# Cross-attention and FP4 feed-forward on one core: three transfers between engines re-ordered, PSUM banks dealt anew

## The chip, the cores and the metric

One core of a Trainium2 chip. Its engines run their own queues in order and wait for one another on semaphores: TensorE (PE, matrix products and transposes), VectorE (DVE), ScalarE (ACT), GpSimd (POOL) and SyncE (SP, which issues the transfers here). PE writes to PSUM, which has eight banks of 128x512 float32; this kernel names all eight. The metric is the device time of one execution in microseconds.

## What is computed

`x` is (4, 1024, 256), the context (4, 154, 192), 16 heads of 64, the hidden width of the feed-forward 704. Cut to what matters:

```python
def xattn(x, context, Wq, Wk, Wv, Wo, bo):           # x is layer-normed
    q, k, v = x @ Wq, context @ Wk, context @ Wv      # 16 heads of 64
    attn = softmax(einsum('bhnd,bhmd->bhnm', q, k) * 64 ** -0.5)
    return merge_heads(attn @ v) @ Wo + bo

def ffn(x, w_gate, w_up, w_down):                     # x is layer-normed
    lin = lambda x, w: fp4(x) @ fp4(w).T              # fp4: quantise and dequantise blocks of 16
    return lin(silu(lin(x, w_gate)) * lin(x, w_up), w_down)

x = x + xattn(layernorm(x), ctx_768, ...)             # its result, a tile of it, is x1 below
x = x + ffn(layernorm(x), ...)
```

## The kernel before, in words

The 4096 rows of `x` are 32 tiles of 128. One *step* works on four tiles at once, at different stages: tile t has its attention computed (16 heads as 8 *pairs* u), tile e = t-1 finishes its attention and gets x1, tile f = t-2 goes through gate and up, tile d = t-3 through down. A step has 8 *slots* k, and each engine has its own list of what it does in slot k, in a fixed order written out in a function `step` per engine. Steps come in pairs (`par` 0 for even tiles, 1 for odd ones); the function `schedule` calls them: six steps in line, a loop over the batches 1 to 3 with four steps that also make K, V and the product B of V and Wo for the new batch (set-ups "v", "k", "roll", "settle") and an inner loop of two pairs of plain steps, and two last steps, then four that only drain.

The products that need more than one float32r pass come as a high part, which ACT copies out of PSUM (`hi_part`), and a low part, which DVE forms as the difference (`lo_part`).

A pair u of heads of tile t passes through the engines so:

- PE, slot u: `scores` (L967) into a bank of PSUM, three products.
- DVE, slot u: `negmax`, the maximum of each head (L782).
- ACT, slot u: exp of the two heads (L610), with sums. Next slot: DVE inverts the sums (L746), POOL multiplies (`normalise`, L472).
- PE, slot u+2: `turn_probs` (L979), which transposes the weights, two blocks of 128 columns for even u and three for odd u, into a bank of PSUM.
- ACT, first work of slot u+3: `weights_hi` makes `pT_hi`. DVE, slot u+3, behind `invert_sums` and ahead of `negmax` of that slot: `weights_lo` makes `pT_lo` (L741 by L637).
- PE, slot u+4, just behind the scores: `attend` (L988), 6 or 9 products with B that gather in the bank `ps_o` over the eight pairs of a tile.

Counts past 7 run on into the next step. When the last `attend` of tile e is done, in slot 3 of step t, DVE adds its result to the input rows: `x1 = xr + ps_o` (L804). The first `attend` of tile t, in slot 4, writes `ps_o` anew and waits for that add. ACT first copies the old `x1` to `y` (L628), before the add may overwrite it.

In the kernel before, the scores of even and odd pairs have a bank each (`ps_s[u % 2]`), so that scores wait for the exp two pairs back; the transposed weights have one bank (`ps_t`), so that `turn_probs(u)` waits for `pT_lo` of pair u-1. PE's order in a slot is: scores, `attend`, `turn_probs`, then transposes for the feed-forward (slots 1, 4, 5), transposes of the next input (slot 6 of even steps), `gate_up` (slots 2 to 5), `down_product` (slot 7), a `q_product` (slots 0, 1, 2, 4 of even steps and 0, 1, 3, 6 of odd ones), the set-up's jobs. In even steps `down_product` waits for `xT_lo`, DVE's work in slot 7 behind `negmax`. DVE's `xqT_lo` (slot 2) and `hqT_lo` (slots 5, 6) stand between `weights_lo` and `negmax`. DVE does the add of x1 in slot 4, behind `negmax` and `q_lo`.

Of the kernel before, what the change touches and what calls it, by code (L numbers as in the profile page):

```python
# [23 lines left out]
def xattn_ffn_kernel(nc: bass.Bass, x, ctx_768, Wq, Wk, Wv, Wo, bo, w_gate, w_up, w_down, out):  # L24
# [29 lines left out]
    with ExitStack() as stack:  # L54
# [69 lines left out]
        ps_t, ps_q, ps_o, ps_m = (bank(n) for n in ("ps_t", "ps_q", "ps_o", "ps_m"))  # L124
        ps_s = [bank("ps_s0"), bank("ps_s1")]
# [4 lines left out]
        def ctx_bank(r):  # L130
            return (ps_s[0], ps_s[1], ps_t, ps_g[0], ps_o)[r]
# [379 lines left out]
        def _(act):  # L511
# [60 lines left out]
            def weights_hi(t, u):  # L572
                if some(PAIRS * t + u - 1):
                    act.wait_ge(o_mm, PAIRS * t + u - 1)
                hi_part(pT[u % 2][0][:, 0:blocks(u), :], parts(ps_t, blocks(u)), (t_mm, PAIRS * t + u + 1), pT_hi)

            def step(pair, par, own=True, before=True, gate=True, down=True, out_=True, ahead=True, queries=True,
# [3 lines left out]
                for k in range(SLOTS):  # L581
# [24 lines left out]
                    if own:  # L606
                        act.wait_ge(max_v, PAIRS * t + k + 1)
                        for s in range(2):
                            h = 2 * k + s
                            ins = act.activation(probs[:, h, 0:M], ps_s[k % 2][:, s * M:(s + 1) * M], ACT.Exp,  # L610
# [12 lines left out]
                    if down and k == 3:  # L623
# [9 lines left out]
        def _(dve):  # L633
# [105 lines left out]
            def weights_lo(t, u):  # L739
                n = blocks(u)  # L740
                lo_part(pT[u % 2][1][:, 0:n, :], parts(ps_t, n), pT[u % 2][0][:, 0:n, :],  # L741
# [19 lines left out]
            def step(pair, par, own=True, before=True, gate=True, down=True, out_=True, ahead=True, queries=True,  # L761
# [3 lines left out]
                for k in range(SLOTS):  # L765
# [14 lines left out]
                    if own:  # L780
                        dve.wait_ge(s_mm, PAIRS * t + k + 1)
                        dve.tensor_reduce(negmax[:, 2 * k:2 * k + 2],  # L782
                                          ps_s[k % 2][:, 0:UM].rearrange("p (h m) -> p h m", h=2),
# [13 lines left out]
                    if before and k == 4:  # L797
                        dve.wait_ge(o_mm, PAIRS * (e + 1))
                        dve.wait_ge(xr_p, e + 1)
                        if some(d + 1):  # L800
                            dve.wait_ge(y_a, d + 1)
                        elif not some(e):
                            dve.wait_ge(raw_mm, RAW_T[3])
                        dve.tensor_tensor(x1[1 - par], xr[1 - par][:, :], ps_o[:, 0:C], ALU.add).then_inc(x1_v, 1)  # L804
# [19 lines left out]
                    if before and k == 5:  # L824
# [6 lines left out]
                        dve.tensor_scalar(xri[:, :], xri[:, :], TIES_DOWN, None, ALU.mult).then_inc(xq_v, 1)  # L831
                    if gate and k == 6:
                        dve.wait_ge(h_v, Q * (f + 1))
                        largest(eh[:, 0:F], hri[:, :], hq_v)
# [18 lines left out]
        def _(pe):  # L853
# [113 lines left out]
            def scores(t, pair, par, u, setup):  # L967
# [3 lines left out]
                if some(PAIRS * t + u - 1):  # L971
                    pe.wait_ge(exp_a, PAIRS * t + u - 1)
                terms = ((1, 0), (0, 1), (0, 0))
                for i, (a, b) in enumerate(terms):
                    ins = pe.matmul(ps_s[u % 2][:, 0:UM], q_sb[a][:, u, par * P:(par + 1) * P], K_sb[b][:, u, :],  # L975
# [3 lines left out]
            def turn_probs(t, u):  # L979
                pe.wait_ge(norm_p, PAIRS * t + u + 1)  # L980
                if some(PAIRS * t + u):
                    pe.wait_ge(pT_lo, PAIRS * t + u)
# [124 lines left out]
```

## Time and profile before

| | |
|---|---|
| median of 3 runs | 984.53 us (983.6 to 984.84) |
| the profiled execution | 986.75 us |
| its span, first to last instruction | 984.9 us |
| PE, DVE, ACT, POOL busy | 857.0, 757.5, 534.0, 529.5 us |
| mean granted TensorE clock | 0.973 of full speed |

The engines overlap, so their busy times don't add up to the span. A row of the view in order of time gives the start of an instruction, its length, engine, line, operation and tiles, and in brackets the idle time of its engine just before and what ended it. Matrix products are pipelined: each is recorded as longer than the distance to the next.

### The profile page before, as it was taken

How to read it: one execution, taken by the hardware profiler on the slowest of the kernel's cores; microseconds unless marked ns; L12 is line 12 of the kernel's file. 1: busy time of each engine (PE TensorE's matmuls, PEld its weight loads, DVE VectorE, ACT ScalarE, POOL GpSimd, SP SyncE). 2: the span in 40 equal slices, each digit the busy share in tenths (PEclk: the TensorE clock that was granted, in tenths of full speed). 3: DMA queues.
4: the chain of work that ended last, by engine and by line, in shares of the span. 5: the costliest groups of instructions: out<-in, count | busy, mean ns of one | idle time of the engine just before them, and what ended most of it. 6: DMA issues, size and time to landing. Idle time of an engine off the chain costs nothing.

```text
span 984.9 us, 21389 instructions
## 1 busy us (share of the span) xinstructions
PE 857.0 (87%) x6254; PEld 812.8 (83%) x6254; DVE 757.5 (77%) x2176; ACT 534.0 (54%) x1879; POOL 529.5 (54%) x677
## 2 busy tenths in 40 slices
PE   4786789999999999989989999989999999999874
PEld 3666789988888998888978888889888888888863
DVE  5857788877778888867878888876877888887762
ACT  4454455556565555556555555556555555655520
POOL 2545666554535656545554656554553656555651
PEclk9888999999999999999999999999999999999986
DMA  7101000001010000001000000001000000000000
GB/s 215 39 11 49 7 17 13 22 13 44 7 33 17 13 23 11 21 14 39 12 28 23 12 22 12 21 8 33 23 7 23 12 18 12 16 11 12 7 11 11
DMA packets 19869, 23.13 MB, mean 23 GB/s; under 512 B 2642, under 2 KB 18234, under 8 KB 19770
## 3 DMA queue, kind: packets, MB, share of 16 engines
q1 hardware_dynamic: 19770, 21.94, 7.2%
q8 instruction: 47, 0.77, 0.3%
q14 instruction: 52, 0.43, 0.1%
HBM read 17.74 MB, written 4.19 MB: 22 GB/s over the span
## 4 chain that ended last, share of the span: by engine, by line
PE 63%; DVE 21%; issue 8%; ACT 4%; POOL 2%; DMA 1%; DVEq 1%; SPq 0%; POOLq 0%; ACTq 0%
PE ps_g L1015 10%; PE ps_q L937 8%; PE ps_s L975 8%; PE ps_t L985 5%; PE ps_o L998 5%; PE ps_o L1000 5%; PE ps_o L999 5%; DVE negmax L782 3%; DVE pT_lo L637 3%; PE ps_m L865 3%; PE ps_g L900 3%; PE ps_m L1025 3%; PE ps_m L1027 2%; PE ps_m L1026 2%; DVE scales L667 2%
## 5 line engine op out<-in xcount | busy, mean ns | idle before, releaser
L472 POOL TENSOR_TENSOR probs<-probs,rsum 128x308 f32<-128x308 f32 x256 | 180.0, 703 | 284.2 <-DVE rsum L746 283.6
L610 ACT ACTIVATE probs<-ps_s,negmax 128x154 f32<-128x154 f32 x512 | 194.7, 386 | 229.4 <-DVE negmax L782 228.2
L998 PE MATMUL ps_o<-B_sb,pT_lo 128*128 128x256 f32 x640 | 183.6, 287 | 38.5 <-DVE x_both L804 33.9
L782 DVE TENSOR_REDUCE negmax<-ps_s 128x2 f32<-128x308 f32 x256 | 121.3, 474 | 78.4 <-PE ps_s L975 76.6
L1000 PE MATMUL ps_o<-B_sb,pT_hi 128*128 128x256 f32 x640 | 181.2, 283 | 0.0
L999 PE MATMUL ps_o<-B_sb,pT_hi 128*128 128x256 f32 x640 | 180.9, 283 | 0.0
L998 PEld LDWEIGHTS ps_o<-B_sb,pT_lo 128*128 128x128 f32 x640 | 121.7, 190 | 45.3 <-issue 42.9
L637 DVE TENSOR_TENSOR pT_lo<-ps_t,pT_hi 128x256 fp32r<-128x256 f32 (+1 forms) x256 | 122.7, 479 | 42.6 <-ACT pT_hi L514 37.4
L985 PE MATMUL ps_t<-ident,probs 128*128 128x128 f32 x640 | 115.0, 278 | 35.9 <-DVE pT_lo L637 35.3
L1015 PE MATMUL ps_g<-WGU,xqT_hi 128*128 128x352 f32 x512 | 136.6, 349 | 3.5 <-DVE B_sb L637 1.9
L514 ACT ACTIVATE pT_hi<-ps_t 128x256 fp32r<-128x256 f32 (+1 forms) x256 | 111.4, 435 | 29.1 <-PE ps_t L985 22.7
L1000 PEld LDWEIGHTS ps_o<-B_sb,pT_hi 128*128 128x128 f32 x640 | 122.1, 191 | 0.0
L999 PEld LDWEIGHTS ps_o<-B_sb,pT_hi 128*128 128x128 f32 x640 | 121.8, 190 | 0.0
L985 PEld LDWEIGHTS ps_t<-ident,probs 128*128 128x128 f32 x640 | 73.8, 141 | 47.3 <-issue 45.7
L610 ACT ACTIVATION_READ_ACCUMULATOR probs<-ps_s,negmax 128x1 f32 x512 | 100.9, 197 | 0.0
L975 PE MATMUL ps_s<-K_hi,q_lo 128*128 128x308 f32 x256 | 87.1, 340 | 3.6 <-issue 3.6
L1015 PEld LDWEIGHTS ps_g<-WGU,xqT_hi 128*128 128x128 f32 x512 | 85.3, 194 | 4.9 <-issue 2.6
L937 PE MATMUL ps_q<-xT_hi,Wq_lo 128*128 128x256 f32 x256 | 80.7, 315 | 8.7 <-DVE q_lo L637 6.1
L1015 PE MATMUL ps_g<-WGU,xqT_lo 128*128 128x352 f32 x256 | 83.5, 326 | 0.0
L441 POOL TENSOR_TENSOR hn<-hn,hc 128x704 f32<-128x704 f32 x32 | 54.4, 1700 | 50.8 <-DVE hc L692 50.8
L975 PE MATMUL ps_s<-K_hi,q_hi 128*128 128x308 f32 x256 | 78.4, 306 | 0.0
L975 PE MATMUL ps_s<-K_lo,q_hi 128*128 128x308 f32 x256 | 78.1, 305 | 0.0
(149 smaller groups left out, 2236.7 us busy)
## 6 DMA issues: line engine op xcount, KB each, us to landing
xa<-in_x_dram SPq DMA_DIRECT2D x33, 128.0 KB, 2.1
xr<-in_x_dram SPq DMA_DIRECT2D x32, 128.0 KB, 2.0
out_dram<-y_xn SPq DMA_DIRECT2D x32, 128.0 KB, 1.7
W_sb<-in_L_xattn_Wk_dram SPq DMA_DIRECT2D x4, 512.0 KB, 4.4
W_sb<-in_L_xattn_Wv_dram SPq DMA_DIRECT2D x3, 512.0 KB, 3.6
probs<-in_L_xattn_Wq_dram SPq DMA_DIRECT2D x1, 1024.0 KB, 7.0
Wo_sb<-in_L_xattn_Wo_dram SPq DMA_DIRECT2D x1, 1024.0 KB, 6.6
VT<-in_ctx_dram SPq DMA_DIRECT2D x1, 384.0 KB
```

The lines of the kernel that those rows point to most:

```text
L472: pool.tensor_tensor(unit, unit, rsum[:, 2 * u:2 * u + 2].unsqueeze(2) .to_broadcast([P, 2, M]), ALU.mult).then_inc(norm_p, 1)
L514: act.activation(dst, src, ACT.Copy).then_inc(done, 1)
L610: ins = act.activation(probs[:, h, 0:M], ps_s[k % 2][:, s * M:(s + 1) * M], ACT.Exp, bias=negmax[:, h:h + 1], accum_out=sums[:, h:h + 1])
L637: dve.tensor_tensor(dst, src, hi.bitcast(F32), ALU.subtract).then_inc(done, 1)
L782: dve.tensor_reduce(negmax[:, 2 * k:2 * k + 2], ps_s[k % 2][:, 0:UM].rearrange("p (h m) -> p h m", h=2), AX_X, ALU.max, negate=True).then_ ...
L937: ins = pe.matmul(ps_q[:, 0:2 * P], Wq_sb[w][:, k, u * P:(u + 1) * P], xT[x_][:, k, :], start=(i == 0), stop=(i == len(terms) - 1))
L975: ins = pe.matmul(ps_s[u % 2][:, 0:UM], q_sb[a][:, u, par * P:(par + 1) * P], K_sb[b][:, u, :], start=(i == 0), stop=(i == len(terms) - 1))
L985: ins = pe.transpose(ps_t[:, j * P:(j + 1) * P], probs_rows[:, at:at + P], ident[:, :])
L998: pe.matmul(ps_o[:, 0:C], lo[:, j, :], w[:, 0:C], start=first, stop=False)
L999: pe.matmul(ps_o[:, 0:C], hi[:, j, :], w[:, C:2 * C], start=False, stop=False)
L1000: ins = pe.matmul(ps_o[:, 0:C], hi[:, j, :], w[:, 0:C], start=False, stop=last)
L1015: ins = pe.matmul(ps_g[q % 2][:, 0:2 * QF], x_[:, k, :], WGU[:, k, a, :, q * QF:(q + 1) * QF], start=(i == 0), stop=(i == len(terms) - 1))
```

## The change

Three things. DVE's add of x1 goes from slot 4, behind `negmax` and `q_lo`, to the end of slot 3; ACT's copy of the old x1 to `y` goes from slot 3 to slot 2. PE's `turn_probs` goes from just behind `attend` to the end of the slot's products, behind the feed-forward's transposes, `gate_up`, `down_product`, `q_product` and the jobs, and ahead of the chunks of raw weights that the first steps turn. The scores now have one bank, so that scores wait for the exp of the pair before; the transposed weights have two, so that `turn_probs(u)` waits for `pT_lo` of pair u-2. The orders of ACT and DVE are otherwise as they were.

```diff
--- before.py
+++ after.py
@@ -121,14 +121,14 @@
         def bank(name):
             return stack.enter_context(nc.psum_tensor(name, [P, 512], F32))
 
-        ps_t, ps_q, ps_o, ps_m = (bank(n) for n in ("ps_t", "ps_q", "ps_o", "ps_m"))
-        ps_s = [bank("ps_s0"), bank("ps_s1")]
+        ps_s, ps_q, ps_o, ps_m = (bank(n) for n in ("ps_s", "ps_q", "ps_o", "ps_m"))
+        ps_t = [bank("ps_t0"), bank("ps_t1")]
         ps_g = [bank("ps_g0"), bank("ps_g1")]
         BANKS = {"q": ps_q, "0": ps_g[0], "1": ps_g[1]}
         FIRST_K = "0101"
 
         def ctx_bank(r):
-            return (ps_s[0], ps_s[1], ps_t, ps_g[0], ps_o)[r]
+            return (ps_s, ps_t[0], ps_t[1], ps_g[0], ps_o)[r]
 
         ld_ctx, ld_w, ld_wkv, ld_wo, ld_wq, ld_bo = (
             sem(n) for n in ("ld_ctx", "ld_w", "ld_wkv", "ld_wo", "ld_wq", "ld_bo"))
@@ -572,7 +572,7 @@
             def weights_hi(t, u):
                 if some(PAIRS * t + u - 1):
                     act.wait_ge(o_mm, PAIRS * t + u - 1)
-                hi_part(pT[u % 2][0][:, 0:blocks(u), :], parts(ps_t, blocks(u)), (t_mm, PAIRS * t + u + 1), pT_hi)
+                hi_part(pT[u % 2][0][:, 0:blocks(u), :], parts(ps_t[u % 2], blocks(u)), (t_mm, PAIRS * t + u + 1), pT_hi)
 
             def step(pair, par, own=True, before=True, gate=True, down=True, out_=True, ahead=True, queries=True,
                      setup=None):
@@ -607,7 +607,7 @@
                         act.wait_ge(max_v, PAIRS * t + k + 1)
                         for s in range(2):
                             h = 2 * k + s
-                            ins = act.activation(probs[:, h, 0:M], ps_s[k % 2][:, s * M:(s + 1) * M], ACT.Exp,
+                            ins = act.activation(probs[:, h, 0:M], ps_s[:, s * M:(s + 1) * M], ACT.Exp,
                                                  bias=negmax[:, h:h + 1], accum_out=sums[:, h:h + 1])
                         ins.then_inc(exp_a, 1)
                     if own and ahead and k == 4:
@@ -620,7 +620,7 @@
                            .then_inc(xln2_a, 1)
                     if turn_at(t, k, 0) is not None:
                         chunk_hi(turn_at(t, k, 0))
-                    if down and k == 3:
+                    if down and k == 2:
                         at = pair - 2 + par
                         act.wait_ge(x1_v, d + 1)
                         if some(at):
@@ -738,7 +738,7 @@
 
             def weights_lo(t, u):
                 n = blocks(u)
-                lo_part(pT[u % 2][1][:, 0:n, :], parts(ps_t, n), pT[u % 2][0][:, 0:n, :],
+                lo_part(pT[u % 2][1][:, 0:n, :], parts(ps_t[u % 2], n), pT[u % 2][0][:, 0:n, :],
                         (pT_hi, PAIRS * t + u + 1), pT_lo)
 
             def invert_sums(t, u):
@@ -780,7 +780,7 @@
                     if own:
                         dve.wait_ge(s_mm, PAIRS * t + k + 1)
                         dve.tensor_reduce(negmax[:, 2 * k:2 * k + 2],
-                                          ps_s[k % 2][:, 0:UM].rearrange("p (h m) -> p h m", h=2),
+                                          ps_s[:, 0:UM].rearrange("p (h m) -> p h m", h=2),
                                           AX_X, ALU.max, negate=True).then_inc(max_v, 1)
                     if out_ and k == 0:
                         dve.wait_ge(d_mm, c + 1)
@@ -795,13 +795,6 @@
                     if turn_at(t, k, 1) is not None:
                         chunk_lo(turn_at(t, k, 1))
                     if before and k == 4:
-                        dve.wait_ge(o_mm, PAIRS * (e + 1))
-                        dve.wait_ge(xr_p, e + 1)
-                        if some(d + 1):
-                            dve.wait_ge(y_a, d + 1)
-                        elif not some(e):
-                            dve.wait_ge(raw_mm, RAW_T[3])
-                        dve.tensor_tensor(x1[1 - par], xr[1 - par][:, :], ps_o[:, 0:C], ALU.add).then_inc(x1_v, 1)
                         if some(e):
                             dve.wait_ge(xln2_a, e)
                         stats(x1[1 - par], st2, mv2, ve2, nm2, (x1_v, e + 1), ln2_v, 5 * e)
@@ -829,6 +822,14 @@
                         fp4_scales(xri[:, :], xsc[:, :], xri[:, :], xq_v, 6 * e)
                         dve.wait_ge(xq_v, 6 * e + 3)
                         dve.tensor_scalar(xri[:, :], xri[:, :], TIES_DOWN, None, ALU.mult).then_inc(xq_v, 1)
+                    if before and k == 3:
+                        dve.wait_ge(o_mm, PAIRS * (e + 1))
+                        dve.wait_ge(xr_p, e + 1)
+                        if some(d + 1):
+                            dve.wait_ge(y_a, d + 1)
+                        elif not some(e):
+                            dve.wait_ge(raw_mm, RAW_T[3])
+                        dve.tensor_tensor(x1[1 - par], xr[1 - par][:, :], ps_o[:, 0:C], ALU.add).then_inc(x1_v, 1)
                     if gate and k == 6:
                         dve.wait_ge(h_v, Q * (f + 1))
                         largest(eh[:, 0:F], hri[:, :], hq_v)
@@ -968,21 +969,21 @@
                 pe.wait_ge(q_lo, PAIRS * pair + u + 1)
                 if setup and setup[0] in ("start", "roll"):
                     pe.wait_ge(k_lo, KV * setup[1] + u // 2 + 1)
-                if some(PAIRS * t + u - 1):
-                    pe.wait_ge(exp_a, PAIRS * t + u - 1)
+                if some(PAIRS * t + u):
+                    pe.wait_ge(exp_a, PAIRS * t + u)
                 terms = ((1, 0), (0, 1), (0, 0))
                 for i, (a, b) in enumerate(terms):
-                    ins = pe.matmul(ps_s[u % 2][:, 0:UM], q_sb[a][:, u, par * P:(par + 1) * P], K_sb[b][:, u, :],
+                    ins = pe.matmul(ps_s[:, 0:UM], q_sb[a][:, u, par * P:(par + 1) * P], K_sb[b][:, u, :],
                                     start=(i == 0), stop=(i == len(terms) - 1))
                 ins.then_inc(s_mm, 1)
 
             def turn_probs(t, u):
                 pe.wait_ge(norm_p, PAIRS * t + u + 1)
-                if some(PAIRS * t + u):
-                    pe.wait_ge(pT_lo, PAIRS * t + u)
+                if some(PAIRS * t + u - 1):
+                    pe.wait_ge(pT_lo, PAIRS * t + u - 1)
                 for j in range(blocks(u)):
                     at = b_at(u, j) * P
-                    ins = pe.transpose(ps_t[:, j * P:(j + 1) * P], probs_rows[:, at:at + P], ident[:, :])
+                    ins = pe.transpose(ps_t[u % 2][:, j * P:(j + 1) * P], probs_rows[:, at:at + P], ident[:, :])
                 ins.then_inc(t_mm, 1)
 
             def attend(t, u, setup):
@@ -1039,10 +1040,6 @@
                         attend(e, k + PAIRS - 4, setup if kind == "settle" else None)
                     if own and k >= 4:
                         attend(t, k - 4, setup if kind in ("start", "roll") else None)
-                    if before and k < 2:
-                        turn_probs(e, k + PAIRS - 2)
-                    if own and k >= 2:
-                        turn_probs(t, k - 2)
                     if gate and k == 1:
                         pe.wait_ge(xq_p, 4 * f + 4)
                         m_free((y_v, d), (xqT_lo, f + 1))
@@ -1073,6 +1070,10 @@
                             pe.wait_ge(q_lo, PAIRS * (pair + par) + max(made))
                     for job in jobs_at(setup, k):
                         make(job, setup[1])
+                    if before and k < 2:
+                        turn_probs(e, k + PAIRS - 2)
+                    if own and k >= 2:
+                        turn_probs(t, k - 2)
                     if turn_at(t, k, 0) is not None:
                         chunk_transposes(turn_at(t, k, 0))
 
```

## Rows read from the trace of the kernel before

**Rows 1.** The page, its line of busy time by engine.

```profile
PE 857.0 (87%) x6254; PEld 812.8 (83%) x6254; DVE 757.5 (77%) x2176; ACT 534.0 (54%) x1879; POOL 529.5 (54%) x677
```

**Rows 2.** The waits: engine, line, releaser; total us, times, longest.

```profile
PE ps_t L985 <- DVE pT_lo L637: 35.3, 40, 3.2
PE ps_o L998 <- DVE x_both L804: 33.9, 28, 2.4
```

**Rows 3.** PE in order of time, an even step; start us, us, instruction.

```profile
610.57 0.31 PE L975 MATMUL ps_s<-K_hi,q_lo 128*128 128x308 f32 x1
...
612.64 0.30 PE L975 MATMUL ps_s<-K_hi,q_lo 128*128 128x308 f32 x1
...
615.38 0.31 PE L975 MATMUL ps_s<-K_hi,q_lo 128*128 128x308 f32 x1
...
618.41 0.30 PE L975 MATMUL ps_s<-K_hi,q_lo 128*128 128x308 f32 x1
...
621.21 0.30 PE L975 MATMUL ps_s<-K_hi,q_lo 128*128 128x308 f32 x1
...
622.79 0.36 PE L998 MATMUL ps_o<-B_sb,pT_lo 128*128 128x256 f32 x1 [0.99 <-DVE x_both L804]
...
623.58 0.38 PE L985 MATMUL ps_t<-ident,probs 128*128 128x128 f32 x2
...
625.81 0.30 PE L975 MATMUL ps_s<-K_hi,q_lo 128*128 128x308 f32 x1
...
634.40 0.38 PE L1025 MATMUL ps_m<-WD,hqT_lo 128*128 128x256 f32 x1 [0.38 <-DVE xT_lo L637]
...
636.64 0.30 PE L975 MATMUL ps_s<-K_hi,q_lo 128*128 128x308 f32 x1
```

**Rows 4.** PE in order of time, the odd step before it.

```profile
585.52 0.31 PE L975 MATMUL ps_s<-K_hi,q_lo 128*128 128x308 f32 x1
...
592.65 0.30 PE L975 MATMUL ps_s<-K_hi,q_lo 128*128 128x308 f32 x1
...
596.16 0.30 PE L975 MATMUL ps_s<-K_hi,q_lo 128*128 128x308 f32 x1
...
598.06 0.36 PE L998 MATMUL ps_o<-B_sb,pT_lo 128*128 128x256 f32 x1 [1.32 <-DVE x_both L804]
...
600.36 0.30 PE L975 MATMUL ps_s<-K_hi,q_lo 128*128 128x308 f32 x1
```

**Rows 5.** ACT in order of time, the even step and the next.

```profile
624.06 0.38 ACT L514 ACTIVATE pT_hi<-ps_t 128x256 fp32r<-128x256 f32 x1 [0.37 <-PE ps_t L985]
...
637.77 0.39 ACT L610 ACTIVATE probs<-ps_s,negmax 128x154 f32<-128x154 f32 x1 [2.76 <-DVE negmax L782]
...
640.77 0.49 ACT L514 ACTIVATE pT_hi<-ps_t 128x384 fp32r<-128x384 f32 x1
```

**Rows 6.** DVE in order of time, the same stretch.

```profile
622.23 0.41 DVE L804 TENSOR_TENSOR x_both<-xr,ps_o 128x256 f32<-128x256 f32 x1
...
624.86 0.56 DVE L637 TENSOR_TENSOR hqT_lo<-ps_m,hqT_hi 128x384 fp32r<-128x384 f32 x1
626.43 0.48 DVE L782 TENSOR_REDUCE negmax<-ps_s 128x2 f32<-128x308 f32 x1 [1.01 <-PE ps_s L975]
...
630.44 0.47 DVE L782 TENSOR_REDUCE negmax<-ps_s 128x2 f32<-128x308 f32 x1
...
633.28 0.47 DVE L782 TENSOR_REDUCE negmax<-ps_s 128x2 f32<-128x308 f32 x1
...
637.26 0.48 DVE L782 TENSOR_REDUCE negmax<-ps_s 128x2 f32<-128x308 f32 x1 [0.66 <-PE ps_s L975]
...
638.65 0.17 DVE L746 RECIPROCAL rsum<-sums 128x2 f32<-128x2 f32 x1 [0.15 <-ACT probs L610]
...
641.77 0.42 DVE L637 TENSOR_TENSOR xqT_lo<-ps_m,xqT_hi 128x256 fp32r<-128x256 f32 x1
```

**Rows 7.** The core, its span and its mean granted clock.

```profile
core 0: 984.9 us, clock 0.973
```

## The prediction

> **What bounds the kernel now.** I read the page first: TensorE (PE) is busy 857.0 us of a span of 984.9, VectorE (DVE) 757.5, ScalarE (ACT) 534.0 [rows 1]. A busy share does not say who waits for whom, so the waits come next. In the whole span PE stands still 35.3 us before the transposes of the weights, for DVE's `pT_lo`, and 33.9 us before the first product of `attend`, for DVE's `x1` [rows 2]. These two are what the change goes for. What it must not lengthen is seen only in the order of time, so I lay the three engines of one ordinary pair of steps beside each other.
>
> Call S(k) the start of PE's scores in slot k and N(k) the start of DVE's `negmax` in that slot. The step of an even tile runs from 610.57 to 636.64, 26.07 us; that of an odd tile from 585.52 to 610.57, 25.05 us [rows 3, 4]. In slots 0 to 3 PE is the last to finish: S goes 2.07, 2.74, 3.03, 2.80 us from slot to slot [rows 3], and DVE's `negmax` starts 0.62 us after the scores (N(5) is 626.43, S(5) 625.81 [rows 3, 6]). In slot 4 PE stands until `x1` is there: the add starts at 622.23 and takes 0.41, and the product starts at 622.79, 0.15 us behind its end [rows 3, 6]. From N(5) on, DVE is the last: N(6) is N(5)+4.01, N(7) is N(6)+2.84, and `down_product`, which needs `xT_lo` in even steps, starts at N(7)+1.12 [rows 3, 6]. So the step is PE-bound in its first half and DVE-bound in its second.
>
> **The change part by part.**
>
> *x1 earlier.* The same 0.41 us instruction runs one slot earlier on DVE, so nothing is added. Queued behind it are `invert_sums(3)` and `pT_lo` of slot 4; these wait for ACT's `pT_hi` anyway, which covers the 0.41 us; without that cover it would cost 0.41. PE's wait in slot 4 goes: it is from the end of the scores to 622.79, about 1.2 us in the even step (621.21+0.43), and 598.06-596.60, about 1.46, in the odd one [rows 3, 4]. ACT's copy of `y` moves a slot ahead with it and has idle time there; I cost it at nothing, at most its own length.
>
> *Transposes last.* The same instructions, the same number. PE no longer waits for the previous `pT_lo` (two banks), and the 35.3 us go from that place. But what hangs on them comes later. ACT's first work in slot k is `pT_hi(k-3)`, and DVE's `pT_lo(k-3)` stands ahead of `negmax(k)` in its queue; the diff leaves both orders as they are. The trace has the lags: the transposes of two blocks start at 623.58 and `pT_hi` at 624.06, 0.48 later [rows 3, 5]. Two transposes take about 0.22 (0.11 each, an estimate from the 18 products that fill 634.40 to 636.64), so `pT_hi` starts 0.26 us after PE is done with the slot. The next DVE instruction behind `pT_lo` starts 0.80 after `pT_hi` for two blocks (624.06 to 624.86) and 1.00 for three (640.77 to 641.77) [rows 5, 6]. So where the transposes end the slot, `negmax` starts 1.06 or 1.26 us after PE is free, not 0.62. In slot 2 `xqT_lo` (0.42) stands between, in slot 5 `hqT_lo` (0.56) [rows 6]: 1.68 and 1.62. The records of DVE overlap the next by a little, so these two are upper ends.
>
> *One bank for the scores.* Scores(k+1) now need exp(k). `negmax` at 637.26 gives exp at 637.77 (+0.51), and DVE sees exp's end at 638.65 (+0.88) [rows 5, 6]. How soon PE starts after an ACT release is in no row of this place; the nearest is 0.15 us after DVE's `x1`. The bounds are 0 and 0.3; I take 0.11, so that S(k+1) is not before N(k)+1.50.
>
> *Sum, even step*, from S(0)=0, with the transposes of the slot before just done:
> N(0)=1.26. S(1) = the later of 2.07 (PE) and 2.76 (exp) = 2.76: a new stall of 0.69. N(1)=3.4 (scores +0.62; `pT_hi` runs right behind exp, whose end by the +0.88 is at 2.65, and `negmax` may start 0.80 after that, at 3.45). S(2)=2.76+2.74=5.50. N(2)=5.50+1.68=7.18. S(3) = the later of 8.53 and 8.68 = 8.68. N(3)=8.53+1.06=9.59. S(4) = the later of 11.48 and 11.09 = 11.48. N(4)=11.40 to 11.48+1.26=12.74. `x1` is there at about N(3)+1.8=11.4, before scores(4) end at 11.9: no wait. S(5)=11.48+(4.60-1.20)=14.88. N(5)=14.88+1.62=16.50. Before, N(5) was 626.43-610.57=15.86: already 0.64 later, though 1.2 was saved. Then as before N(6)=20.51 and N(7)=23.35. Scores(7) wait for exp(6) to 22.0, which hides, since PE then waits for `xT_lo`: down starts at 24.47, takes 2.24, and the transposes, now behind it, 0.33: the next S(0) is 27.04. That is +0.97 us.
>
> *Odd step*: the same to S(3)=8.68; slot 3 is 3.51 long (596.16-592.65 [rows 4]), S(4)=12.19, N(4)=13.45, S(5) = the later of 12.19+4.20-1.46=14.93 and 14.95, N(5)=16.55, N(6)=20.56, S(7)=22.06 by exp. The scores and three blocks of `attend` take about 1.5 (an estimate, 0.12 a product), down 2.24, transposes 0.33: 26.13, that is +1.08.
>
> Sixteen of the 32 steps with scores of their own are of these two kinds. Mean +1.0 each: +16 us. In the other steps (the first two, the four that make K, V and B of each batch, the last two) slots are longer, so the exp wait often hides while the `x1` gain stays. Bounds: each gains 1.2 (-19 in all) or loses 1.0 (+16). I take 0: the long slots gain, the short ones among them lose. The sum is 984.9+16, about 1001; the profiled execution itself took 986.75, the median of the runs is 984.53, so **1000** in the runs' terms.
>
> A rule that speaks against the change: DVE's `negmax` starts with the scores' bank at 637.26 and ACT's exp holds it to about 638.6, while in the kernel before PE may fill the other bank [rows 5, 6]. The Trainium skill, "Perfetto Trace Analysis", section "Matmuls", says that independent groups should rotate through different PSUM banks, so that emptying one overlaps the next group's matmuls. By that rule alone the scores would lose their overlap and the transposes gain it. No figure follows from it here.
>
> **The rivals.**
> *Faster.* The lag behind the transposes doesn't reach `negmax` (N stays at S+0.62). Then S goes 0, 2.12, 4.86, 7.89, 10.69, 14.09 and N(5)=14.71, 1.15 us earlier than before; 0.33 is given back behind down. 28 steps had the wait [rows 2]: 28x0.8, about 962 us. For it: PE's records show these two waits as its largest. Against: `pT_lo` is ahead of `negmax` in DVE's queue. The point from which it decides: slots 0, 2 and 5 each hand their lag on, so if each lag were 0.33 us shorter than I have it (N(0) at S(0)+0.93), the even step would come out even, and below that the kernel is faster.
> *Nothing to measure.* Gain and lag cancel, 983 to 986, for instance when the twelve setup and edge steps gain all of their 1.2.
> *Dearer than forecast.* Scores(7) at N(6)+1.5 and slot 6 meet more late work on DVE (its second half is full), or `x1` is late in slot 3 and PE keeps about 0.5 us of its wait: another 0.5 to 0.8 a step on 28, 1015 to 1023.
> *The clock falls.* PE stands more often. With waits of 1.3 us in each step the granted clock stays at its upper level (mean 0.973 over the run [rows 7]); were half of the matmuls to run at 1.2 GHz, hundreds of us would be lost. I see no gap longer than about 1.5 us in the sum.
>
> **How the numbers follow.** Forecast (986.5 to 1015): 0.70. Dearer: 0.12, with the clock in it 0.02. Even: 0.05. Faster: 0.13, most of it near 962 to 982. The median of this kernel is told from no change at about 0.2%, 2 us. So slower 0.82, same 0.05, faster 0.13. The range leaves out 2 in 10: from the lower edge of "even" to the middle of "dearer", 980 to 1019. The likeliest case's own is 988 to 1013.
>
> **What would show it.** Right: PE's waits for `x1` and `pT_lo` are gone from the list; in their place PE waits before scores for ACT's exp, in slots 0 and 7 above all, and DVE's waits for `pT_hi` grow; N(0) near S(0)+1.3, N(5) near S(5)+1.6, N(5) to N(6) still 4.0; steps near 27.0 and 26.1. Wrong: N near S+0.62 in slots 0, 4 and 5, or slot 7 shorter than now, or steps of the batch set-up that lose several us, which I did not lay out slot by slot.

## The result

The changed kernel took 1022.25 us at the median (1021.7 to 1026.87 in four executions; a fifth took 1018.79), against 984.1 for the kernel before on the same chip: a ratio of 1.0388 (95% interval 1.0352 to 1.0424; the brackets behind later ratios are such intervals). It is slower, as forecast, but by 38 us and not by 16, and outside the range of 980 to 1019. The profiled execution has a span of 1025.0 us, 40.1 more than before; all lengths of steps and stretches below are from such profiled executions. Its mean granted clock is 0.974, where it was 0.973 [rows 7].

The page's line of busy time of the changed kernel, which answers to [rows 1]:

```profile
PE 872.4 (85%) x6254; PEld 815.3 (80%) x6254; DVE 722.9 (71%) x2176; ACT 524.4 (51%) x1879; POOL 530.5 (52%) x677
```

DVE and ACT do the same work in less busy time and a longer span. The waits of the changed kernel (engine, line, releaser; total us, times, longest):

```profile
ACT pT_hi L514 <- PE ps_t L986: 220.4, 175, 4.5
...
DVE pT_lo L637 <- ACT pT_hi L514: 196.2, 160, 3.3
...
PE ps_s L976 <- ACT probs L610: 44.9, 53, 2.4
...
PE ps_g L1016 <- DVE xqT_lo L637: 14.6, 28, 1.0
...
PE ps_o L999 <- DVE x_both L832: 0.9, 1, 0.9
```

PE's two waits of [rows 2] are gone: 0.9 us are left of the 33.9 for `x1`, and none for `pT_lo` before the transposes. In their place ACT stands 220.4 us for the transposes and DVE 196.2 us for `pT_hi`. In the kernel before, these two lines are:

```profile
DVE pT_lo L637 <- ACT pT_hi L514: 37.4, 61, 3.6
...
ACT pT_hi L514 <- PE ps_t L985: 22.7, 34, 2.2
```

PE itself shows new waits: for exp before the scores, and before the feed-forward's products for `xqT_lo` (1.6 us in the kernel before).

An even step of plain kind on PE in order of time, which answers to [rows 3]: scores of slots 0 to 5, with `gate_up` of slot 2 at 641.42; `down_product` at 659.09; and scores of the next step.

```profile
634.14 0.39 PE L976 MATMUL ps_s<-K_hi,q_lo 128*128 128x308 f32 x1
...
636.83 0.41 PE L976 MATMUL ps_s<-K_hi,q_lo 128*128 128x308 f32 x1 [0.38 <-ACT probs L610]
...
639.59 0.39 PE L976 MATMUL ps_s<-K_hi,q_lo 128*128 128x308 f32 x1
...
641.42 0.59 PE L1016 MATMUL ps_g<-WGU,xqT_hi 128*128 128x352 f32 x2 [0.45 <-DVE xqT_lo L637]
...
643.34 0.39 PE L976 MATMUL ps_s<-K_hi,q_lo 128*128 128x308 f32 x1
...
646.13 0.39 PE L976 MATMUL ps_s<-K_hi,q_lo 128*128 128x308 f32 x1
...
649.51 0.39 PE L976 MATMUL ps_s<-K_hi,q_lo 128*128 128x308 f32 x1
...
659.09 0.39 PE L1026 MATMUL ps_m<-WD,hqT_lo 128*128 128x256 f32 x1 [0.79 <-DVE xT_lo L637]
...
661.58 0.39 PE L976 MATMUL ps_s<-K_hi,q_lo 128*128 128x308 f32 x1
```

The same step on DVE, `negmax` of slots 0 to 5 with the add of `x1` in between, and `negmax` of the next step, which answers to [rows 6]:

```profile
635.42 0.47 DVE L782 TENSOR_REDUCE negmax<-ps_s 128x2 f32<-128x308 f32 x1
...
637.55 0.48 DVE L782 TENSOR_REDUCE negmax<-ps_s 128x2 f32<-128x308 f32 x1
...
641.21 0.47 DVE L782 TENSOR_REDUCE negmax<-ps_s 128x2 f32<-128x308 f32 x1
...
644.44 0.47 DVE L782 TENSOR_REDUCE negmax<-ps_s 128x2 f32<-128x308 f32 x1
...
645.78 0.41 DVE L832 TENSOR_TENSOR x_both<-xr,ps_o 128x256 f32<-128x256 f32 x1
...
647.48 0.47 DVE L782 TENSOR_REDUCE negmax<-ps_s 128x2 f32<-128x308 f32 x1
...
651.12 0.47 DVE L782 TENSOR_REDUCE negmax<-ps_s 128x2 f32<-128x308 f32 x1
...
662.93 0.47 DVE L782 TENSOR_REDUCE negmax<-ps_s 128x2 f32<-128x308 f32 x1
```

Subtract S(0)=634.14 and set it beside the sum of the prediction. N(0) is 1.28 (said: 1.26), S(1) 2.69 (2.76), N(1) 3.41 (3.4), S(2) 5.45 (5.50), N(2) 7.07 (7.18), S(3) 9.20 (8.68), N(3) 10.30 (9.59), N(4) 13.34 (12.74), S(5) 15.37 (14.88), N(5) 16.98 (16.50), the next S(0) 27.44 (27.04). Scores(1) stand behind exp, and `negmax` starts 1.28 to 1.62 us after the scores in slots 0, 2, 4 and 5, not 0.62. In slot 7 the wait of the scores hides, since PE waits 0.79 us for `xT_lo` behind them. So the mechanism of the prediction is in these rows. What is not in them is the other 24 us of 40.1; the experiments place them.

### The profile page after: what moved, and what is told of

Same layout as the page of the kernel before. It is cut to its first block, busy times and chain, and to the rows that moved or that the text cites. A ratio compares the mean times of both kernels' runs of the same rounds, so it can differ in the third digit from the quotient of the medians.

```text
span 1025.0 us, 21403 instructions
## 1 busy us (share of the span) xinstructions
PE 872.4 (85%) x6254; PEld 815.3 (80%) x6254; DVE 722.9 (71%) x2176; ACT 524.4 (51%) x1879; POOL 530.5 (52%) x677
## 4 chain that ended last, share of the span: by engine, by line
PE 53%; DVE 23%; ACT 10%; issue 9%; POOL 2%; DVEq 1%; DMA 0%; ACTq 0%; POOLq 0%; SPq 0%
PE ps_g L1016 9%; PE ps_q L938 6%; PE ps_s L976 6%; PE ps_t L986 5%; DVE negmax L782 5%; ACT pT_hi L514 4%; DVE pT_lo L637 4%; PE ps_o L999 4%; PE ps_o L1001 4%; ACT probs L610 4%; PE ps_o L1000 4%; PE ps_m L1026 3%; PE ps_g L901 2%; PE ps_m L866 2%; PE ps_m L1028 2%
## 5 line engine op out<-in xcount | busy, mean ns | idle before, releaser
L637 DVE TENSOR_TENSOR pT_lo<-ps_t,pT_hi 128x256 fp32r<-128x256 f32 (+1 forms) x256 | 124.1, 485 | 198.5 <-ACT pT_hi L514 196.2
L514 ACT ACTIVATE pT_hi<-ps_t 128x256 fp32r<-128x256 f32 (+1 forms) x256 | 112.0, 437 | 221.1 <-PE ps_t L986 220.4
L1016 PE MATMUL ps_g<-WGU,xqT_hi 128*128 128x352 f32 x512 | 133.2, 341 | 20.4 <-DVE xqT_lo L637 14.6
L976 PE MATMUL ps_s<-K_hi,q_lo 128*128 128x308 f32 x256 | 101.1, 395 | 49.1 <-ACT probs L610 44.9
L986 PE MATMUL ps_t<-ident,probs 128*128 128x128 f32 x640 | 112.5, 274 | 0.0
L976 PEld LDWEIGHTS ps_s<-K_hi,q_lo 128*128 128x128 f32 x256 | 48.9, 191 | 63.2 <-ACT probs L610 34.7
L938 PE MATMUL ps_q<-xT_hi,Wq_lo 128*128 128x256 f32 x256 | 77.0, 301 | 12.5 <-DVE q_lo L637 6.6
L986 PEld LDWEIGHTS ps_t<-ident,probs 128*128 128x128 f32 x640 | 80.9, 142 | 3.7 <-issue 0.2
L453 POOL TENSOR_TENSOR small<-small 128x1 f32<-128x1 f32 x65 | 36.4, 559 | 88.4 <-DVE small L664 88.4
```

What stands on the lines that cost most here:

```text
L514: act.activation(dst, src, ACT.Copy).then_inc(done, 1)
L637: dve.tensor_tensor(dst, src, hi.bitcast(F32), ALU.subtract).then_inc(done, 1)
L938: ins = pe.matmul(ps_q[:, 0:2 * P], Wq_sb[w][:, k, u * P:(u + 1) * P], xT[x_][:, k, :], start=(i == 0), stop=(i == len(terms) - 1))
L976: ins = pe.matmul(ps_s[:, 0:UM], q_sb[a][:, u, par * P:(par + 1) * P], K_sb[b][:, u, :], start=(i == 0), stop=(i == len(terms) - 1))
L986: ins = pe.transpose(ps_t[u % 2][:, j * P:(j + 1) * P], probs_rows[:, at:at + P], ident[:, :])
L1016: ins = pe.matmul(ps_g[q % 2][:, 0:2 * QF], x_[:, k, :], WGU[:, k, a, :, q * QF:(q + 1) * QF], start=(i == 0), stop=(i == len(terms) - 1))
```

## The experiments

Each is timed beside the kernel before, which took 983.9 us in the first set, 985.5 in the second and 984.0 in the third; ratios are to those. The expectations weigh two theories. The *lag theory*: the late transposes make `pT_hi` and `pT_lo` late, and these stand ahead of `negmax` in DVE's queue. The *bank theory*: the cost is that the scores have one bank. The *loop theory*, of one later expectation, joins them: the one bank hands the late exp on to the next scores.

**x1 early alone.** From the diff, the parts that move the copy of `y` on ACT and the add, with its waits, on DVE (`...` marks lines left out, here and below):

```diff
-                    if down and k == 3:
+                    if down and k == 2:
                         at = pair - 2 + par
...
                     if before and k == 4:
-                        dve.wait_ge(o_mm, PAIRS * (e + 1))
...
-                        dve.tensor_tensor(x1[1 - par], xr[1 - par][:, :], ps_o[:, 0:C], ALU.add).then_inc(x1_v, 1)
...
+                    if before and k == 3:
+                        dve.wait_ge(o_mm, PAIRS * (e + 1))
...
+                        dve.tensor_tensor(x1[1 - par], xr[1 - par][:, :], ps_o[:, 0:C], ALU.add).then_inc(x1_v, 1)
```

> The kernel before with the add of x1 (and ACT's copy of y) moved alone. Both theories agree here: PE's 33.9 us of waits for x1 go and nothing else is delayed, about 1.1 us in each of 28 steps, 945 to 962 us. If DVE's full second half eats the gain, 970 to 984.

Measured: 943.66 us, ratio 0.9595 (0.9572 to 0.9617), just below the 945 to 962 that I gave. The wait was worth what it showed, and a little more: 40 us saved, of which 33.9 stand as PE's wait in [rows 2].

**Transposes last alone.**

```diff
-                    if before and k < 2:
-                        turn_probs(e, k + PAIRS - 2)
-                    if own and k >= 2:
-                        turn_probs(t, k - 2)
...
                     for job in jobs_at(setup, k):
                         make(job, setup[1])
+                    if before and k < 2:
+                        turn_probs(e, k + PAIRS - 2)
+                    if own and k >= 2:
+                        turn_probs(t, k - 2)
```

> The kernel before with the transposes of the weights moved to the end of the slot alone; banks and x1 as before. Lag theory (late transposes make pT_hi and pT_lo late, and these stand ahead of negmax): negmax starts 1.1 to 1.6 us after the scores in slots 0 to 5, and the step grows by 1.5 to 2 us, since x1 and its wait come later too: 1015 to 1045 us. Bank theory (the one bank of the scores is the cost): 975 to 990 us.

Measured: 1085.73 us, ratio 1.1043 (1.1 to 1.1086). The direction is the lag theory's; the size, 102 us, is beyond the 31 to 61 that I gave. One part of the surplus is in PE's wait for `x1`:

```profile
PE ps_o L998 <- DVE x_both L804: 51.0, 28, 2.8
```

With the add still behind a `negmax` that is late, this wait is 51.0 us and not 33.9. That is 17 of the 102 us. Another part is in the clock: the mean granted clock of this run is 0.955, against 0.973 in the kernel before. The last section has the rows.

**Banks alone.**

```diff
-        ps_t, ps_q, ps_o, ps_m = (bank(n) for n in ("ps_t", "ps_q", "ps_o", "ps_m"))
-        ps_s = [bank("ps_s0"), bank("ps_s1")]
+        ps_s, ps_q, ps_o, ps_m = (bank(n) for n in ("ps_s", "ps_q", "ps_o", "ps_m"))
+        ps_t = [bank("ps_t0"), bank("ps_t1")]
...
-                if some(PAIRS * t + u - 1):
-                    pe.wait_ge(exp_a, PAIRS * t + u - 1)
+                if some(PAIRS * t + u):
+                    pe.wait_ge(exp_a, PAIRS * t + u)
```

> The kernel before with the banks dealt anew alone (one for the scores, two for the transposed weights); order and x1 as before. Lag theory: scores need exp of the pair before, that is S(k) + 0.62 + 1.5 = 2.1 us, and no slot of PE is shorter, but for scores(7), which come later while PE no longer waits for pT_lo behind them: 980 to 990 us. Bank theory: 1000 us or more.

Measured: 987.34 us, ratio 1.0032 (1.0012 to 1.0051). PE's wait for exp in it:

```profile
PE ps_s L975 <- ACT probs L610: 25.7, 34, 2.4
```

PE now waits 25.7 us for exp, and the 35.3 us for `pT_lo` are gone: one wait has taken the other's place. The bank theory falls. The edit takes a bank from the scores and gives it to the transposes, so the 3 us are the net of both; what either half costs or gives alone, no run here shows. The Trainium skill's rule that independent groups should rotate through different PSUM banks ("Perfetto Trace Analysis", section "Matmuls") speaks on both sides of this edit, and the two waits agree with it: the group that lost its second bank now waits, and the one that gained a bank no longer does.

**x1 early and banks.** The changed kernel with `turn_probs` put back behind `attend`.

> The changed kernel with the transposes put back just behind attend: x1 early and the new banks. Lag theory: the gain of x1 stays whole, 945 to 962 us. Bank theory: 1000 us or more.

Measured: 948.14 us, ratio 0.9633 (0.9607 to 0.9658). As the lag theory had it, the gain of `x1` stays. So the one edit that is missing here, the place of the transposes, costs 74 us on top (1022.25 against 948.14).

**x1 early and transposes last, banks as before.**

> x1 early and the transposes last, with the banks as before (two for the scores, one for the transposed weights). Loop theory: the late transposes cost most of what they cost because the one bank of the scores hands the late exp on to the next scores; without it S(1) is bound by PE again, the plain steps come out about 1 us shorter than the changed kernel's, 985 to 1005 us. If the late transposes cost as much with two banks, 1015 to 1030 us.

Measured: 1007.53 us, ratio 1.0238 (1.0206 to 1.027): 2.5 us above what I gave for the loop theory and 7.5 below its rival, so neither range holds it. The late transposes cost 64 us with two banks for the scores (943.66 to 1007.53), and the new banks add 15 to that where they cost 3 to 5 with early transposes. So most of the cost comes without the new banks. In plain steps these add to it by kind: an even step takes 27.33 us here and 27.51 in the changed kernel, an odd one 24.94 and 25.81.

**Transposes early in set-up steps alone.** In the changed kernel, the four steps of each batch that make K, V and B (and the first two) have `turn_probs` behind `attend` again.

```diff
+                    if setup:
+                        if before and k < 2:
+                            turn_probs(e, k + PAIRS - 2)
+                        if own and k >= 2:
+                            turn_probs(t, k - 2)
...
                     for job in jobs_at(setup, k):
                         make(job, setup[1])
-                    if before and k < 2:
-                        turn_probs(e, k + PAIRS - 2)
-                    if own and k >= 2:
-                        turn_probs(t, k - 2)
+                    if not setup:
+                        if before and k < 2:
+                            turn_probs(e, k + PAIRS - 2)
+                        if own and k >= 2:
+                            turn_probs(t, k - 2)
```

> The changed kernel with the transposes put back behind attend in the steps that make K, V and B alone; plain steps as changed. If the unforeseen +18 us of the profile's twelve set-up steps come from late transposes, these steps fall to their lengths with x1 early alone, about 35 us less in all: 984 to 992 us. If they come from the one bank or from the jobs' own waits, 1005 us or more.

Measured: 987.68 us, ratio 1.0035 (1.0013 to 1.0058). For the four set-up steps of a batch take `negmax` of slot 0 where the first begins and where the step behind the fourth begins. These are the pairs for all three batches, first in the kernel before and then in the changed one:

```profile
212.09 0.48 DVE L782 TENSOR_REDUCE negmax<-ps_s 128x2 f32<-128x308 f32 x1
...
333.08 0.48 DVE L782 TENSOR_REDUCE negmax<-ps_s 128x2 f32<-128x308 f32 x1
...
437.90 0.48 DVE L782 TENSOR_REDUCE negmax<-ps_s 128x2 f32<-128x308 f32 x1
...
560.08 0.48 DVE L782 TENSOR_REDUCE negmax<-ps_s 128x2 f32<-128x308 f32 x1
...
664.68 0.47 DVE L782 TENSOR_REDUCE negmax<-ps_s 128x2 f32<-128x308 f32 x1
...
785.38 0.48 DVE L782 TENSOR_REDUCE negmax<-ps_s 128x2 f32<-128x308 f32 x1
```

```profile
218.51 0.47 DVE L782 TENSOR_REDUCE negmax<-ps_s 128x2 f32<-128x308 f32 x1
...
346.69 0.47 DVE L782 TENSOR_REDUCE negmax<-ps_s 128x2 f32<-128x308 f32 x1
...
455.24 0.47 DVE L782 TENSOR_REDUCE negmax<-ps_s 128x2 f32<-128x308 f32 x1
...
582.09 0.47 DVE L782 TENSOR_REDUCE negmax<-ps_s 128x2 f32<-128x308 f32 x1
...
690.79 0.48 DVE L782 TENSOR_REDUCE negmax<-ps_s 128x2 f32<-128x308 f32 x1
...
817.97 0.47 DVE L782 TENSOR_REDUCE negmax<-ps_s 128x2 f32<-128x308 f32 x1
```

Before, the set-ups take 120.99, 122.18 and 120.70 us; in the changed kernel 128.18, 126.85 and 127.18: 7.2, 4.7 and 6.5 more, 18.3 in all. In the kernel of this experiment, batch 2:

```profile
441.27 0.48 DVE L782 TENSOR_REDUCE negmax<-ps_s 128x2 f32<-128x308 f32 x1
...
557.50 0.48 DVE L782 TENSOR_REDUCE negmax<-ps_s 128x2 f32<-128x308 f32 x1
```

It takes 116.23 us, 10.6 less than in the changed kernel and less than before: with `x1` early alone this stretch takes 116.44. So the set-up steps, which I had costed at nothing, hold 18.3 of the 40.1 us, and it is the late transposes there that cost them. They cost more than 18.3, since they also eat the gain of `x1`: the whole experiment is 35 us below the changed kernel.

**Results of the set-up first.** ACT and DVE take `q`, K and B ahead of `pT_hi` and `pT_lo` in set-up steps. ACT's part of the edit, where it adds them (DVE's is alike, and both leave them out at their old place):

```diff
+                    if setup:
+                        if own and queries and q_unit(par, k - 1) is not None:
+                            q_hi_part(pair + par, q_unit(par, k - 1))
+                        for job in jobs_before(setup, k):
+                            take_hi(job, setup[1])
                     if before and k < 3:
                         weights_hi(e, k + PAIRS - 3)
```

> The changed kernel, but in set-up steps ACT and DVE take the high and low parts of q, K and B ahead of pT_hi and pT_lo, not behind them. If the set-up steps are long because these parts stand behind the late pT_hi, pT_lo and negmax and PE waits for them, its waits for K_lo, B_sb and q_lo shrink and the time falls by 4 to 12 us, 1010 to 1018. If it is the scores' chain alone (pT_hi, pT_lo, negmax, exp, scores), negmax comes later still and the time is 1022 us or more.

Measured: 1023.0 us, ratio 1.0392 (1.0358 to 1.0427): no different from the changed kernel, so the 4 to 12 us that I gave for this order don't come. The reason for trying it was in "roll" of the changed kernel, PE in order of time:

```profile
518.02 2.15 PE L901 MATMUL ps_g<-Wo_sb,VT 128*64 128x256 f32 x10 [0.92 <-DVE K_lo L648]
520.00 0.38 PE L986 MATMUL ps_t<-ident,probs 128*128 128x128 f32 x2
...
528.14 0.59 PE L1016 MATMUL ps_g<-WGU,xqT_hi 128*128 128x352 f32 x2 [1.76 <-DVE B_sb L637]
```

PE stands 0.92 us for K's low part and 1.76 for B's. With the parts taken first these two waits are gone from the stretch of batch 2, and the time is the same. What the new order gives in some steps it takes in others: by `negmax`, the steps "roll" and "settle" of batch 2 are 1.4 and 1.3 us shorter than in the changed kernel, "v" and "k" 0.9 and 2.0 us longer. So this experiment doesn't show that the two waits cost nothing; it shows that this order doesn't win them back.

**Transposes ahead of the jobs.** In the changed kernel `turn_probs` goes ahead of the set-up's jobs, still behind everything that plain steps have.

```diff
                     if own and queries and q_unit(par, k) is not None:
                         q_product(pair + par, q_unit(par, k))
+                    if before and k < 2:
+                        turn_probs(e, k + PAIRS - 2)
+                    if own and k >= 2:
+                        turn_probs(t, k - 2)
                     if kind == "v" and k < 2:
                         pe.wait_ge(h_v, Q * f)
```

> The changed kernel with the transposes ahead of the set-up's jobs, still behind everything else in the slot. Plain steps as changed. If in set-up steps the transposes are late because the jobs (up to 2 us of PE) stand ahead of them, the set-up steps lose 3 to 8 us in each of the three batches: 998 to 1013 us. If the work that plain steps have too is what makes them late, 1018 to 1024 us.

Measured: 1005.64 us, ratio 1.0221 (1.0187 to 1.0256). The set-up of batch 2 by `negmax`:

```profile
443.45 0.47 DVE L782 TENSOR_REDUCE negmax<-ps_s 128x2 f32<-128x308 f32 x1
...
566.09 0.47 DVE L782 TENSOR_REDUCE negmax<-ps_s 128x2 f32<-128x308 f32 x1
```

122.64 us, 0.5 more than before. The place behind the jobs is half of what the set-up steps paid for: 520.00 in the rows of "roll" above is the transposes of slot 0, which start only when ten products of the jobs, from 518.02 on, have been issued. The other half is the place behind the slot's other products, which plain steps have too: the stretch is still 6.4 us longer than with the transposes early (122.64 against 116.23). Over the three batches the set-ups take 382.2 us in the changed kernel, 364.4 here and 344.9 with the transposes early.

**`pT_lo` behind `negmax`.** The changed kernel; DVE's call of `weights_lo` goes from ahead of `negmax` to behind it.

```diff
-                    if before and k < 3:
-                        weights_lo(e, k + PAIRS - 3)
-                    if own and k >= 3:
-                        weights_lo(t, k - 3)
...
                                           AX_X, ALU.max, negate=True).then_inc(max_v, 1)
+                    if before and k < 3:
+                        weights_lo(e, k + PAIRS - 3)
+                    if own and k >= 3:
+                        weights_lo(t, k - 3)
```

> The changed kernel with DVE's pT_lo behind negmax in every slot, not ahead of it. If pT_lo in front of negmax is what lengthens the steps, negmax is back at about 0.62 us after the scores in slots 0, 1, 3, 4 and the plain steps lose 0.8 to 1.2 us each, the set-up steps some too: 985 to 1003 us. If not, within 5 us of the changed kernel.

Measured: 1007.27 us, ratio 1.0225 (1.0178 to 1.0271), outside what I gave, by 4 us. Scores and `negmax` of slots 0 and 2 of an even step, PE first and then DVE:

```profile
334.48 0.39 PE L976 MATMUL ps_s<-K_hi,q_lo 128*128 128x308 f32 x1
...
339.66 0.39 PE L976 MATMUL ps_s<-K_hi,q_lo 128*128 128x308 f32 x1
```

```profile
335.20 0.46 DVE L778 TENSOR_REDUCE negmax<-ps_s 128x2 f32<-128x308 f32 x1
...
341.08 0.47 DVE L778 TENSOR_REDUCE negmax<-ps_s 128x2 f32<-128x308 f32 x1
```

In slot 0 `negmax` is back at 0.72 us behind the scores. In slot 2 it is still at 1.42, since `xqT_lo` stands ahead of it and needs `xqT_hi`, which ACT makes behind the late `pT_hi` (DVE stands 1.70 us for it there). So the queue of ACT holds up DVE by a second way, which I had left out when I wrote the expectation; 15 of the 38 us come back.

**Two tries at a faster kernel**, both on `x1` early alone. What is left there in slot 5 is DVE's wait for `xn`, which ACT makes behind exp. First, at the end of slot 4:

```diff
-                    if before and k == 5:
+                    if before and k == 4:
```

> x1 early alone (943.7 us), and ACT normalises x1 into xn at the end of slot 4, not behind exp in slot 5, so that DVE need not wait for it (19 us of waits). If the second half of a step is bound by DVE, 925 to 938 us; if ACT's pT_hi in slot 5 is held up by the wait for POOL, 945 us or more.

Measured: 954.86 us, ratio 0.9697 (0.9667 to 0.9728), 11 us slower than without it. ACT's wait for it:

```profile
ACT y_xn L619 <- POOL small L455: 22.2, 32, 3.1
```

ACT stands 22.2 us for POOL in all, and `pT_hi` of the next slot is queued behind it: DVE's wait for `pT_hi` is 67.2 us here and 33.9 with `x1` early alone. Second, in slot 5 behind `hqT_hi` and ahead of `q_hi`, tanh and exp:

```diff
                         hi_part(hqT[0][:, 3 * r:3 * r + 3, :], parts(ps_m, 3), (hqT_mm, 2 * d + r + 1), hqT_hi)
+                    if before and k == 5:
+                        act.wait_ge(ln2_p, 2 * e + 2)
...
+                        act.activation(xn, x1[1 - par], ACT.Identity, bias=nm2[:, :], scale=rs2[:, :])\
+                           .then_inc(xln2_a, 1)
```

> x1 early alone (943.7 us), and ACT makes xn in slot 5 behind hqT_hi and ahead of q_hi, tanh and exp, where it stood idle for 0.5 to 1.2 us and POOL's part is done. DVE's wait for xn (0.55 to 0.9 us a step, 19 us in all) goes: 922 to 936 us. If xn is not ready there and holds up ACT, 945 us or more.

Measured: 928.99 us, ratio 0.9444 (0.9411 to 0.9477). DVE between two `negmax` in slots 5 and 6 of an even step, with `x1` early alone and then with `xn` first:

```profile
602.95 0.48 DVE L782 TENSOR_REDUCE negmax<-ps_s 128x2 f32<-128x308 f32 x1 [0.27 <-PE ps_s L976]
...
604.94 0.42 DVE L667 TENSOR_REDUCE scales<-y_xn 128x16 f32<-128x256 f32 x1 [0.55 <-ACT y_xn L619]
...
606.96 0.47 DVE L782 TENSOR_REDUCE negmax<-ps_s 128x2 f32<-128x308 f32 x1
```

```profile
585.20 0.48 DVE L782 TENSOR_REDUCE negmax<-ps_s 128x2 f32<-128x308 f32 x1 [0.27 <-PE ps_s L976]
...
586.54 0.41 DVE L667 TENSOR_REDUCE scales<-y_xn 128x16 f32<-128x256 f32 x1
...
588.56 0.47 DVE L782 TENSOR_REDUCE negmax<-ps_s 128x2 f32<-128x308 f32 x1
```

The 0.55 us before the maximum over `xn` are gone, and the distance of the two `negmax` goes from 4.01 to 3.36. This version beats both kernels, and its time lies in the range that I gave.

## Why the prediction was wrong in size

*What bounds the kernel, and the gain of `x1`*: right. The wait was in each of 28 steps, and its removal alone gives 40 us, where the 1.2 to 1.46 us a step that I took make 37.

*The lag of late transposes*: right in kind and, in the sum of the plain steps, in size, the latter partly by luck. N(0), N(2) and N(5) stand 1.28, 1.62 and 1.61 us behind their scores, where I had 1.26, 1.68 and 1.62, scores(1) stand behind exp as forecast, and PE starts the scores 1.41 us after `negmax` (635.42 to 636.83), not 1.50. One term was left out: `gate_up` in slot 2 needs `xqT_lo`, which is late with the rest, and PE stands there 0.45 us (641.42). One was too large: two transposes take 0.14 us and three 0.24 (643.20 to 643.34 and 661.34 to 661.58 in the changed kernel), where I had 0.22 and 0.33. The even step is 27.44 long and not 27.04; the odd steps are 25.8 by `negmax` where I had 26.13. The even steps are dearer than I had them and the odd ones cheaper, and the two misses nearly cancel. Sixteen plain steps make +16.3 us in the two traces, where the sum had +16; the rows of the set-ups show eight of them, four behind each of the first two (346.69 to 455.24 and 582.09 to 690.79, 217.25 us, against 209.42 before: +0.98 a step).

*The other steps, taken at nothing*: this is the step that failed. I wrote that their slots are longer, "so the exp wait often hides while the `x1` gain stays", with bounds of -19 to +16 us. They cost 24: 18.3 in the twelve set-up steps, and about 5.5 before the first and behind the last plain step. The longer slots did not hide the lag. Against the kernel with `x1` early alone, the set-up steps lose 3.0 us each and the plain steps 2.2, while `x1` gives 1.4 and 1.2 back. Half of the loss in the set-ups is the place behind the jobs: they make these slots long, and the transposes had been put behind them. The step "roll" alone, which has the most jobs, holds 9.2 of the 18.3 us. With the transposes ahead of the jobs the set-ups are at their old length (+0.5 in batch 2), and with the transposes early in these steps alone the kernel is at 987.68, 35 us less. The other half is the lag that plain steps have too; it is also in "settle", which has no jobs and is 1.25 us longer than before. I had read the line of the diff that puts `turn_probs` behind `make(job)`, and did not count what stands before it. The upper bound was wrong for the same reason: it took the loss of a plain step as the most that a step can lose. The prediction did name set-up steps that lose several us as a sign that it is wrong, and as what it had not laid out.

*The rivals*: "dearer than forecast" is where the time fell, near its upper end (1022.25, of 1015 to 1023), but by neither of its two mechanisms: `x1` is not late, and the wait of scores(7) hides as I said. So a time inside that rival's range is no support for it. The even case fell too; it speaks of twelve set-up and edge steps, where the sum counts sixteen. The faster rival fell on the row that I gave as its test, N(0) at 1.28 and not below 0.93. The clock of the changed kernel is as it was, 0.974 against 0.973.

*What the one bank does*: in the sum it sets S(1) and S(3), through exp. The kernels with the old banks and with the new put the whole deal of banks at 3 us alone and 15 with late transposes, beside the 64 to 74 that the transposes cost. With late transposes they differ by 0.2 us in an even plain step and by 0.9 in an odd one, but with the old deal PE stands for `pT_lo` instead (16.9 us in the kernel with the transposes last), so no run gives the price of the chain through exp alone.

Late transposes with `x1` late cost 102 us rather than the 64 with `x1` early. Of the 38 between them, PE's longer wait for `x1` accounts for 17 and falls of the clock for about 15 by the estimate of the last section; the other 6 are open. Of the about 5.5 us at the two ends, 2.4 lie before the first plain step and 3.1 behind the last. They were not looked into further, but for this: with the transposes ahead of the jobs the first plain step starts 5.4 us sooner (its `negmax` at 107.87 and not 113.28).

## What to carry to other kernels

Before an instruction is moved to the end of its engine's slot, look at who is first in line for it on the next engines: a consumer at the head of an in-order queue holds back all that stands behind it, and the wait shows on an engine that was idle enough to look harmless. Lay out the steps that are not typical as well, slot by slot: it is there that "the end of the slot" can mean a different place. And of several edits in one change, time each alone: here one was worth -40 us, one +3, and one +64 to +102, by what else was changed.

## What the runs showed that I had not expected

PE resumes quickly behind ACT: the exp of the slot starts 0.5 us after `negmax`, and scores start 1.41 us after it. In the changed kernel's 53 waits of this kind PE starts 0.05 to 0.15 us behind the end of ACT's last record of the exp, so the release by ACT costs PE no more than DVE's 0.15 us [rows 3, 6].

Waits of PE can cost clock. In the kernel with the transposes last alone the mean granted clock is 0.955, against 0.973 before. Between 200 us and the start of the last step with scores it falls fourteen times from the upper level, 2.4 GHz, to the lower, 1.2 GHz, for a few us each; in the kernel before and in the changed kernel it falls once there, with `x1` early and the transposes last three times. Each of these falls comes just behind a wait of PE, of 1.76 to 3.21 us; in eight of the fourteen it is the wait for `x1`. One of them, PE in order of time and then stretches of 2 us (the figure behind POOL's is the granted clock):

```profile
346.01 0.36 PE L998 MATMUL ps_o<-B_sb,pT_lo 128*128 128x256 f32 x1 [1.94 <-DVE x_both L804]
```

```profile
346.00:348.00 2.00, 1.99 (x11) 2.00 (x12) 1.45 (x8) 0.58 (x3) 0.97 (x3) 0.69 0.19 66
348.00:350.00 2.00, 2.00 (x9) 1.93 (x9) 0.00 (x0) 0.06 (x1) 0.42 (x1) 0.50 0.00 0
```

This is in the step "settle" of batch 1, which takes 30.15 us by `negmax`; the same step of batches 2 and 3 has no fall and takes 28.77 and 28.78. So a fall costs about 1.4 us here. The eleven more than with `x1` early are then worth about 15 us, an estimate from these steps. Not every such wait has a fall behind it: other waits of 1.94 us for `x1` have none.
